# Turning the states' output of 22 attention steps by way of DRAM, in a new order of stages

## The reference

```python
q, k, v = heads(x @ Wq), heads(x @ Wk), heads(x @ Wv)
s = clip(heads(x @ Ws), -32, 32)
z = cumlogsumexp(s, axis=time)
p, g = exp(s - z), exp(previous(z) - z)
# over time t, for each head
hk = hk * g[t] + outer(k[t], p[t]);  ok[t] = (q[t] * scale) @ hk
pv = softmax(ok, axis=-1)                      # over the 64 slots
hv = hv * g[t] + outer(p[t], v[t]);  ov[t] = pv[t] @ hv
o = ov * rsqrt(mean(ov**2) + EPS) * g_norm_weight * silu(x @ Wg)
y = o @ Wo
```

## Time and profile before

| | |
|---|---|
| median of 2 runs | 1484.72 us |
| the profiled execution | 1485.11 us |
| its span | 1483.3 us |
| TensorE busy | 1448.3 us, 98% |
| VectorE busy | 1091.2 us, 74% |
| ScalarE busy | 637.7 us, 43% |
| GpSimd busy | 435.9 us, 29% |
| DMA | 166.53 MB, mean 112 GB/s |

### The profile page before, as it was taken

How to read it: one execution, slowest core, us unless ns; L and a number is a source line. 1 busy time by engine, 2 the same in 40 slices (tenths; PEclk the granted TensorE clock), 3 DMA queues, 4 the chain that set the end, 5 groups by cost and what they waited for, 6 DMA issues and landing times.

```text
span 1483.3 us, 23970 instructions
## 1 busy us (share of the span) xinstructions
PE 1448.3 (98%) x9240; PEld 1167.8 (79%) x9240; DVE 1091.2 (74%) x2062; ACT 637.7 (43%) x1205; POOL 435.9 (29%) x283
## 2 busy tenths in 40 slices
PE   8999999999999999999999999999999999999998
PEld 6888888888888888888888888878888646666675
DVE  5567766666667777777677687688787886977788
ACT  4333333333324333333333334234343466776775
POOL 0311011211205445435554423221421343333320
PEclk9999999999999999999999999999999999999999
DMA  4554433443524444435555311101211225444452
GB/s 158 176 138 128 120 97 104 124 119 94 152 71 136 118 139 132 132 110 130 163 157 165 118 44 51 51 8 36 78 44 35 88 79 184 122 129 144 154 172 92
DMA packets 213297, 166.53 MB, mean 112 GB/s; under 512 B 89664, under 2 KB 174528, under 8 KB 213184
## 3 DMA queue, kind: packets, MB, share of 16 engines
q1 hardware_dynamic: 191920, 133.27, 30.4%
q10 hardware_dynamic: 21264, 31.73, 7.2%
HBM read 115.02 MB, written 49.94 MB: 111 GB/s over the span
## 4 chain that ended last, share of the span: by engine, by line
PE 85%; DVE 7%; DMA 2%; POOL 2%; ACT 2%; issue 1%; SPq 0%; POOLq 0%; ACTq 0%; DVEq 0%
PE bank L490 17%; PE bank L496 17%; PE bank L493 17%; PE bank L723 6%; PE bank L618 4%; PE bank L738 4%; PE bank L759 3%; PE bank L580 2%; PE bank L553 2%; PE bank L604 2%; DVE AM L1198 1%; PE bank L575 1%; PE bank L561 1%; PE bank L588 1%; DVE OKM L1176 1%
## 5 line engine op out<-in xcount | busy, mean ns | idle before, releaser
L490 PE MATMUL bank<-Wh,X 128*128 128x512 f32 x512 | 205.6, 402 | 0.1
L496 PE MATMUL bank<-Wh,X 128*128 128x512 f32 x512 | 200.0, 391 | 0.0
L493 PE MATMUL bank<-Wl,X 128*128 128x512 f32 x512 | 199.3, 389 | 0.0
L490 PE MATMUL bank<-X,Wh 128*128 128x512 f32 x384 | 156.4, 407 | 6.3 <-ACT Wh L816 6.3
L1512 POOL TENSOR_TENSOR Wl<-RAW,Wh 128x512 fp32r<-128x512 f32 (+1 forms) x65 | 112.1, 1734 | 135.9 <-ACT Wh L816 135.8
L496 PE MATMUL bank<-X,Wl 128*128 128x512 f32 x384 | 150.8, 393 | 0.0
L493 PE MATMUL bank<-X,Wh 128*128 128x512 f32 x384 | 150.2, 391 | 0.0
L1535 POOL TENSOR_TENSOR sm<-sm,half 128x8 f32<-128x8 f32 x31 | 51.0, 1647 | 328.1 <-DVE sm L1223 328.1
L1558 POOL TENSOR_TENSOR LO<-M,HI 128x512 fp32r<-128x512 f32 x64 | 82.6, 1291 | 160.3 <-PE bank L732 128.0
L878 ACT ACTIVATE V<-bank 128x256 f32<-128x256 f32 x128 | 48.7, 381 | 182.1 <-PE bank L496 181.8
L723 PE MATMUL bank<-XT,W 128*128 128x512 bf16 x512 | 121.9, 381 | 0.6 <-DVE GS L1381 0.6
(11 more groups left out here) (223 smaller groups left out, 3280.9 us busy)
## 6 DMA issues: line engine op xcount, KB each, us to landing
z_scratch<-EV SPq DMA_DIRECT2D x64, 256.0 KB, 2.0
Z<-z_scratch SPq DMA_DIRECT2D x16, 1024.0 KB, 5.8
o_scratch<-OG ACTq DMA_DIRECT2D x96, 128.0 KB, 2.4
AM<-o_scratch ACTq DMA_DIRECT2D x24, 512.0 KB, 4.7
RAW<-wgT SPq DMA_DIRECT2D x16, 512.0 KB, 4.6
RAW<-wuT SPq DMA_DIRECT2D x16, 512.0 KB, 4.4
RAW<-wdT SPq DMA_DIRECT2D x16, 512.0 KB, 4.4
RAW<-Wo SPq DMA_DIRECT2D x14, 512.0 KB, 4.4
```

Of the source, the lines that this page charges most:

```text
L490: engine.matmul(o, lh(c), rh(c), start=c == 0, stop=False)
L493: engine.matmul(o, lh(c), rl(c), start=False, stop=False)
L496: last = engine.matmul(o, ll(c), rh(c), start=False, stop=c == n - 1)
```

## The change

OKM of the steps 2 to 23 takes the way of DRAM too. VectorE writes it with 32-column blocks grouped, ScalarE's queue stores it in four parts in stage ok (`states_out`) and loads it into OKN in a new stage `load_m` (`states_in`), VectorE transposes the blocks back into OKM, where maximum, subtraction and exponential now work in place; TensorE's four transposes of these steps are gone, and those of turn_w read OKM. The running sum becomes the stage `scan`. `ALONE` gets another order: ok and sums follow q, s comes before k, vg0 and vg1 stand before turn_w, scores and weights directly behind it, then scan and vg2, values and vg3, and y at the end. `STEP` keeps its order with scan where it was. `HOLD` has some other numbers. Counters are merged (hk_evac into hk_add, w3_clip into w3_made), VectorE's masks in weights wait for o_lo, and SyncE issues e_out before k_out, and both loads after vg0.

```diff
-ALONE = ("states", "q", "k", "tern", "ok", "sums", "load_x", "turn_ok", "s", "turn_og", "vg0", "turn_w", "turn_o",
-        "tern", "vg1", "vg2", "tern", "y", "scores", "weights", "turn_k", "turn_e", "values", "keys", "vg3")
-STEP = ("states", "q", "k", "tern", "load_x", "ok", "sums", "turn_o", "s", "turn_ok", "vg0", "turn_w", "tern", "vg1",
-        "y", "vg2", "scores", "weights", "values", "keys", "tern", "vg3")
-OF_NEXT = ("q", "k", "s", "vg0", "vg1", "vg2", "vg3", "keys", "scores", "turn_e", "turn_k")
+ALONE = ("states", "q", "ok", "sums", "load_x", "s", "load_m", "k", "tern", "turn_ok", "turn_og", "vg0", "vg1",
+        "turn_w", "turn_o", "tern", "scores", "weights", "scan", "vg2", "turn_k", "turn_e", "values", "keys", "vg3",
+        "tern", "y")
+STEP = ("states", "q", "k", "tern", "load_x", "ok", "sums", "turn_o", "s", "turn_ok", "vg0", "turn_w", "tern", "scan",
+        "vg1", "y", "vg2", "scores", "weights", "values", "keys", "tern", "vg3")
+OF_NEXT = ("q", "k", "s", "vg0", "scan", "vg1", "vg2", "vg3", "keys", "scores", "turn_e", "turn_k")
...
                 elif stage == "turn_ok":
+                    if moved(n):
+                        return
                     bk = take(("okt", n), (S["ok_less_max"], n + 1))
...
+            def states_out(n):
+
+                act.wait_ge(S["ok_norm"], n + 1)
+                act.wait_ge(S["m_in"], 16 * (n - 2))
+                src = OKM[:].rearrange("p (b x) -> p b x", b=4)
+                to = way_m.rearrange("(b r) (a x) -> r b a x", b=4, a=4)
+                for a in range(4):
+                    engine.dma_start(to[:, :, a], src[32 * a:32 * a + 32]).then_inc(S["m_stored"], 16)
+
+            def states_in(n):
+                act.wait_ge(S["m_stored"], 64 * (n - 1))
+                act.wait_ge(S["ok_turned"], n)
+                act.wait_ge(S["w_turned"], min(n, 2))
+                act.wait_ge(S["ok_totals"], 6)
+                engine.dma_start(OKN[:], way_m).then_inc(S["m_in"], 16)
...
+                elif stage == "scan":
+                    dve.wait_ge(S["e_exp"], n + 1)
+                    dve.wait_ge(S["w_evac"], n)
+                    dve.wait_ge(S["const_in"], 16)
+                    engine.tensor_tensor_scan(ZT[:], ONE[:, 0:1].broadcast_to([128, 512]), ET[:, par, :], 0.0,
+                                              ALU.mult, ALU.add).then_inc(S["z_scan"], 1)
+                    dve.wait_ge(S["z_scan"], n + 1)
+                    engine.reciprocal(ZT[:], ZT[:]).then_inc(S["z_recip"], 1)
...
                 elif stage == "ok":
                     dve.wait_ge(S["ok_sum"], n + 1)
                     dve.wait_ge(S["ok_turned"], n)
-                    engine.tensor_tensor(OKM[:], bank("ok", n)[:], ZT[:], ALU.mult).then_inc(S["ok_norm"], 1)
+                    dve.wait_ge(S["w_turned"], n)
+                    if moved(n):
+                        engine.tensor_tensor(OKB, split_32(bank("ok", n)[:]), split_32(ZT[:]),
+                                             ALU.mult).then_inc(S["ok_norm"], 1)
+                    else:
+                        engine.tensor_tensor(OKM[:], bank("ok", n)[:], ZT[:], ALU.mult).then_inc(S["ok_norm"], 1)
                 elif stage == "turn_ok":
-                    bk = g8(bank("okt", n)[:])
+                    if moved(n):
+                        okt = okn = g8(OKM[:])
+                        dve.wait_ge(S["m_in"], 16 * (n - 1))
+                        engine.transpose(OKM[:].rearrange("p (i a c) -> p a i c", i=4, a=4),
+                                         OKN[:].rearrange("p (a i c) -> p a i c", a=4, i=4)).then_inc(S["ok_turned"], 1)
+                    else:
+                        okt, okn = g8(bank("okt", n)[:]), g8(OKN[:])
...
                 if stage == "s" and moved(n):
-                    sends += [(place, sent, n) for sent in ("e_out", "k_in", "e_in")]
+                    sends.append((place, "e_out", n))
+                if stage == "vg0" and moved(n):
+                    sends += [(place, "k_in", n), (place, "e_in", n)]
```

66 lines of the change are left out of this document (36 added, 30 removed).

## The result

The changed kernel takes 1531.15 us (median of 2 runs, 1530.05 to 1532.25) against 1484.72: a ratio of 1.0306, 95% interval [1.0290, 1.0322], 3.1% slower. The profiled execution has a span of 1530.4 us (before: 1483.3). The forecast was 1507, 22 us more than before; it became 46. The sign is right, the size of the loss is off by a factor of two.

A forecast was written before the change was run, and what follows sets the result against it. TensorE was taken to bound the kernel, with VectorE becoming an equally long second chain. Terms -10 (transposes), +22 (Wo), +6 (GpSimd), +4 (late loads) sum to +22 on 1484.72: 1507 us, range 1475 to 1535.

The forecast's parts named there:

- the sum for Wo: Wo's scaling and rounding stand before HK's copy at step end: 2.3 us in eight steps, late Wo loads in two, +22.
- The four transposes, -10: TensorE loses OKM's transposes: 0.80 us a step saved, 0.35 returned waiting for WT at the weights, 22 steps: -10 us.
- and takes 1.75: The ok matmuls at the step's end, after the HK adds: 1.75 us, making VectorE's chain 33.25 a step.
- VectorE as a second bound: VectorE's row from WT's start through the HK adds: 18.66 us, making its chain 33.25 against TensorE's 33.33 a step.
- w: Time in a step, from the states' product's end, when VectorE starts WT: 12.8 us as long as M is below 8.6.
- GpSimd, +6: GpSimd's clamp of the second ternary task slows VectorE's second OTl subtraction in 12 steps: between 0 and 10, taken +6 us.
- Late loads, +4: Loads of the states' output later than 8.6 us into a step: 0.2 us a step, +4 us.
- M: Time in a step, from the states' product's end, when OKN is fully loaded: 8.3 us, limit 8.6.
- TensorE stays the bound: Rival: slack in HK's copy or VectorE's row leaves only the -10: 1475, or 1467 without waiting at the weights; chance 0.2.
- The load comes late: Rival: stores and loads go one after the other, M 10.3, 37 us in place of 4: 1540; chance 0.15.
- GpSimd blocks for the whole instruction: Rival: VectorE is delayed up to the clamp's 3.9 us in 12 steps, 47 in place of 6: 1548; chance 0.05.

The follow-up runs named there:

- the run at 1489.62: Changed kernel with Wo moved, AM's load behind OKN's, early scan, clamp held, ET/KT stores on ScalarE's queue, Kt/Et loads ahead of a raw load: 1489.62 us, ratio 1.0023.
- the run that gained 9: Changed kernel with the output weights (Wo) of seven weight changes made behind the next step's K projection: 1521.95 us, ratio 1.0238.
- 25 us against 9 and 1: Changed kernel with Wo moved and AM's load behind OKN's: 1506.48 us, 25 less; Wo alone behind K 1521.95, AM's load alone 1529.87.

## Why the prediction had the sign right and the size wrong

The chains of waits that the forecast names are the ones that lengthened the kernel. What failed is their pricing. The step that failed most is the sum for Wo: it took 2.3 us of chain for the whole cost and put TensorE's clock behind the wait at nothing. The loads were priced by their average although only the late steps count, the gain of the four transposes was put too high and the clamp too low. Each step can be split at WT's start, the end of the HK adds, the first ok matmul and the scaling. Against the ordinary step 3 (12.78, 18.66, 0.16 and 1.97 us) the 42.1 us of steps 2 to 23 fall apart as follows:

| part | forecast | measured |
|---|---|---|
| ordinary steps, for the four transposes | -10 | -4.5 |
| Wo's chain in front of HK, seven steps | 20 | 18.6 |
| TensorE's clock behind it | 0 | 6.3 |
| the clamp beside OTl | 6 | 9.5 |
| WT starting later than 12.78 | 4 | 10.1 |
| VectorE's waits for Et | 0 | 1.4 |
| rest | | 0.7 |

Outside, step 1 and step 24 took 5.2 where the forecast had 2.3.

**The four transposes, -10: wrong in size, -4.5.** I let 0.80 go and 0.35 come back. TensorE's timeline in the run at 1489.62, where TensorE is the bound of a step:

```profile
571.61 0.83 PE L595 MATMUL bank<-V,Et 128*64 128x128 f32 x12
572.37 0.50 PE L517 MATMUL bank<-X,Wh 128*128 128x512 f32 x1
...
583.43 0.60 PE L624 MATMUL bank<-C,OKM 128*128 128x128 f32 x4
583.96 1.16 PE L580 MATMUL bank<-QP,KT 64*128 64x128 f32 x16
...
585.49 1.16 PE L633 MATMUL bank<-WT,ET 64*128 64x128 f32 x16 [0.37 <-DVE WT L1263]
```

And in TensorE's timeline of the kernel before, behind the sums of the earlier trace rows, which start at 504.54, the next projection:

```profile
505.91 0.48 PE L490 MATMUL bank<-X,Wh 128*128 128x512 f32 x1
```

The forecast took the end of the sums (505.36, modelled) and the 506.16 of the chain; by starts the distance from the sums to the next projection, 1.37, became 0.76: 0.61 saved and not 0.80. The weights' transposes (511.48 to 511.83 before) take 0.53 in place of 0.35, and the scores until the weights (522.94 to 523.93) 1.53 in place of 0.99, of which 0.37 is the wait for WT: 0.72 given back and not 0.35. The products behind them start closer to each other by 0.2 in all, so this step takes 33.60 from sums to sums in place of 33.72: 0.1 gained. The transposes and scores took 0.18 and 0.17 more in their new neighbourhood, without a wait. Why is open. On VectorE's side, "and takes 1.75" measured 2.12 from the end of the HK adds to the scaling (33.57 against 33.25).

**VectorE as a second bound: right**, to 0.02 us in w and in the 18.66; the run with the early scan shows it from the other side.

**Wo, +22: the chain is right, the clock was missing.** 2.3 us of chain in eight steps as forecast, and waits of 1.4 and 1.1 for the raw Wo in two (2.0 forecast). Missing is TensorE's clock: after five of the seven waits of 2.1 to 4.4 us the ok matmuls ran at the lower level, which cost 6.3 us; after two (2.07 and 2.82 us) they did not. In the run without transfer, where no late load of OKN mixes in, the seven steps lose 27 with the clock; step 24 loses another 3.5.

**GpSimd, +6: 9.5.** The full 0.84 in 11 of 12 steps; between my bounds I had taken the middle, though both starts fell together. Without the clamp the scan took some of it over.

**Late loads, +4: 10.1.** M was 8.56 on average, under the 8.6 at which it should begin to cost, but it scatters by 3 us, and only the late steps count: with M at 9.92, 9.34 or 10.25 WT starts 4.3 later, at 14.20, 13.63 and 14.54. Nine such steps make 7.3 of the 10.1. An average compared with a limit hides this. In the other steps WT is late by something else (17, 21 and 23, with M at 8.5 and less). Without the transfer the window is 5.2 us shorter.

**Not seen:** step 1, 1.7: VectorE waits 1.28 for Et there.

**The rivals.** *TensorE stays the bound*: no, ok waits for HK wherever something disturbs. *The load comes late*: M stayed under the 9.2 at which it decides. *GpSimd blocks for the whole instruction*: the pair takes 2.12 beside a clamp of 3.68. The Trainium skill, SBUF — State Buffer, section Summary: rules for kernel authors, says that of a VectorE instruction with two inputs in SBUF and a GpSimd one that reads it the second to issue "fully blocks" until the first finishes. Beside the clamp, one input, the traces don't agree: OTl lost 0.84, as the scan of before had. Beside Wol, two inputs, the trace agrees: 2.04 lost of 2.34. The same skill's DMA: Bandwidth & Descriptors, section Anatomy of one DMA, has a fit of 2.0 us and 1 us for each 436 KB, measured on GpSimd's path; 2.6 us for 256 KB is an estimate from it. OKN's load takes that, 2.6, when AM's is behind it, and 3.4 when AM's is ahead; AM's 512 KB take 3.6 and 4.4, above the 3.2 that the same estimate gives.

What stays open is what makes the clock fall behind one wait of 2 to 3 us and not behind another, and what makes WT late where OKN's load was in time.

## What to carry to other kernels

Moving work off the bound engine pays only if what replaces it in the order doesn't lengthen the next chain: here the way through DRAM gave 4 to 6 us and the order that came with it took 49. Look at every queue for what the moved stage now stands in front of (a weight's rounding in front of the copy on which the next product waits), and read single steps, not totals: the run that gained 9 had gained 19 in six steps and lost 7 in two others. When a stall of 2 us or more on TensorE can't be removed, allow for its clock as well as its length: here 0.9 us a stall on average, 1.6 at most. Price a load by the steps in which it is late, not by its average. And before two edits are called more than their sum, see whether they are still the same edits: 25 us against 9 and 1 came mostly from Wo's new place in two steps.

## What the runs showed of the hardware

- TensorE's granted clock. In the changed kernel TensorE waited for HK for 2.11, 2.79, 4.35, 2.80 and 4.00 us ahead of five ok products, was at the lower level (0.50 of its clock) for all or part of them, and they took up to 1.6 us longer. After waits of 2.07 and 2.82 us in the same execution the clock stayed at 1.00, and after the waits of up to 0.54 us in other steps too. Eight products without use in the gap left one of seven such places at the lower level, and the seven steps took 6.7 us less.
- Two loads on one queue, 512 KB and 256 KB. With the large one issued 1.9 us ahead they take 3.6 and 3.4 us; with the small one issued 0.5 us ahead, 4.4 and 2.6.
- An operation of VectorE with both inputs in SBUF that starts up to 0.35 us behind GpSimd's clamp of one input loses 0.84 us, though the clamp lasts 3.7. One that starts 0.15 us behind GpSimd's Wol with its two inputs loses 2.04 us, of Wol's 2.34 (twice, in the run at 1521.95).
